# Every engine's program written out for all eight batches in place of a loop over two

## The reference

```python
xn = layernorm(x)
q, k, v = xn @ wq + bq, xn @ wk + bk, xn @ wv + bv      # 16 heads of 16
q, k = rope(q), rope(k)
s = softmax(q @ k.T / 4 + causal) @ v @ wo + bo
g = silu(ffn(xn))            # (silu(xn @ wg.T) * (xn @ wu.T)) @ wd.T, hidden size 768, int weights / 127
x = x + s * g
```

## Time and profile before

| | |
|---|---|
| time, median of 3 runs | 725.07 us (724.32 to 727.4) |
| the profiled execution, first to last instruction | 726.0 us |
| PE busy | 677.4 us, 93% |
| VectorE, ScalarE, GpSimd busy | 538.6, 411.4, 351.7 us |
| mean granted TensorE clock of that execution | 0.962 of full speed |

### The profile page before, as it was taken

How to read it: one execution, slowest core, us unless ns; L and a number is a source line. 1 busy time by engine, 2 the same in 40 slices (tenths; PEclk the granted TensorE clock), 3 DMA queues, 4 the chain that set the end, 5 groups by cost and what they waited for, 6 DMA issues and landing times.

```text
span 726.0 us, 15898 instructions
## 1 busy us (share of the span) xinstructions
PE 677.4 (93%) x4452; PEld 455.3 (63%) x4452; DVE 538.6 (74%) x1735; ACT 411.4 (57%) x897; POOL 351.7 (48%) x697
## 2 busy tenths in 40 slices
PE   1779999999999999899999999899999999999995
PEld 0656766676667665576656766568666766567653
DVE  3779678966978688675889669676697858886663
ACT  2446467756566447464476565555656644765671
POOL 1055493547625674336745476244762567422240
PEclk9888999999999999699999999879999999999898
DMA  8200000000100002000020001100020000100010
GB/s 247 78 1 1 31 1 1 2 3 1 62 28 1 1 1 89 6 1 2 1 89 2 2 1 59 35 2 3 1 74 16 1 1 2 60 1 1 1 60 29
DMA packets 16425, 18.15 MB, mean 25 GB/s; under 512 B 576, under 2 KB 15936, under 8 KB 16320
## 3 DMA queue, kind: packets, MB, share of 16 engines
q1 hardware_dynamic: 15232, 15.86, 6.8%
q10 hardware_dynamic: 1088, 1.05, 0.4%
HBM read 12.71 MB, written 4.19 MB: 23 GB/s over the span
## 4 chain that ended last, share of the span: by engine, by line
PE 84%; DVE 5%; issue 3%; ACT 3%; DMA 2%; POOL 1%; ACTq 0%; DVEq 0%; POOLq 0%
PE ps_w L487 34%; PE ps_w L565 12%; PE ps_w L554 12%; PE ps_o L580 11%; PE ps_w L536 7%; PE ps_w L542 3%; PE ps_w L589 3%; DMA rot<-L_attn_wo 2%; ACT probs L668 1%; PE ps_w L501 1%; ACT o_t L672 1%; DVE ps_w L778 1%; DVE h_lo L719 1%; PE ps_w L595 1%; DVE at_lo L801 1%
## 5 line engine op out<-in xcount | busy, mean ns | idle before, releaser
L778 DVE CUSTOM_DVE_ANT_0 ps_w<-ps_w,cst 128x512 f32<-128x512 f32 (+3 forms) x512 | 242.8, 509 | 54.5 <-PE ps_w L554 52.7
L668 ACT ACTIVATE probs<-ps_w 128x512 f32<-128x512 f32 (+1 forms) x384 | 194.1, 535 | 116.5 <-PE ps_w L565 113.6
L869 POOL TENSOR_SCALAR_AFFINE_SELECT probs<-probs 128x128 f32<-128x128 f32 (+1 forms) x384 | 130.7, 347 | 259.8 <-ACT probs L668 257.4
L565 PE MATMUL ps_w<-q_st,k_st 64*128 64x512 f32 (+3 forms) x512 | 137.9, 375 | 3.7 <-DVE at_lo L801 1.8
L554 PE MATMUL ps_w<-k_st,q_st 48*128 48x512 f32 (+3 forms) x512 | 139.3, 370 | 1.5 <-issue 0.8
L565 PEld LDWEIGHTS ps_w<-q_st,k_st 64*128 64x128 f32 x512 | 72.1, 189 | 52.9 <-issue 29.0
L658 ACT CAST q_st<-ps_w 128x512 fp32r<-128x512 f32 x128 | 74.6, 589 | 51.4 <-PE ps_w L542 39.3
L554 PEld LDWEIGHTS ps_w<-k_st,q_st 48*128 48x128 f32 x512 | 73.6, 189 | 47.3 <-issue 35.4
L487 PE MATMUL ps_w<-xt_hi,wgu_hi 128*128 128x512 f32 x192 | 89.3, 465 | 6.5 <-issue 4.8
L580 PE MATMUL ps_o<-probs,vals 128*32 128x512 f32 (+3 forms) x1024 | 92.5, 451 | 2.0 <-POOL probs L869 2.0
L487 PE MATMUL ps_w<-xt_lo,wgu_hi 128*128 128x512 f32 x192 | 80.7, 420 | 0.0
(11 more groups left out here) (91 smaller groups left out, 1178.2 us busy)
## 6 DMA issues: line engine op xcount, KB each, us to landing
xn<-L_attn_x SPq DMA_DIRECT2D x8, 512.0 KB, 4.8
res<-L_attn_x SPq DMA_DIRECT2D x8, 512.0 KB, 4.3
result<-res SPq DMA_DIRECT2D x8, 512.0 KB, 2.9
probs<-L_ffn_w_gate SPq DMA_DIRECT2D x1, 768.0 KB, 12.4
probs<-L_ffn_w_up SPq DMA_DIRECT2D x1, 768.0 KB, 14.2
probs<-L_ffn_w_down SPq DMA_DIRECT2D x1, 768.0 KB, 15.1
cst<-shape_constants SPq DMA_DIRECT2D x1, 384.0 KB, 5.1
rot<-L_attn_wq ACTq DMA_DIRECT2D x1, 256.0 KB, 4.2
```

The lines of the kernel that those rows point to most:

```text
L565: last = pe.matmul(dst[:, col:col + w], k_st[rows, pair % 4, kt * P:(kt + 1) * P], q_st2[rows, pair % 2, kt * P:SEQ], start=True, stop=True)
L668: nc.scalar.activation(probs[:, (pair % 2) * SLOTS + slot, col:col + WIDTH[c]], w_of(item)[:, 0:WIDTH[c]], ACT.Exp, scale=QSCALE).then_inc ...
L778: last = nc.vector.tensor_tensor_reduce(out=w_of(item)[:, col:col + w], in0=w_of(item)[:, col:col + w], in1=cst[:, C_MASK + SEQ - w:C_MASK ...
L869: nc.gpsimd.affine_select(out=v, in_=v, compare_op=ALU.is_ge, fill=0.0, base=0, pattern=pattern, channel_multiplier=-1).then_inc(masked_do ...
```

## The change

The program of each engine is written out for all batches: `run` goes through the prologue and batches 0 to 8 with no loop, and SyncE's loop is a Python loop as well. All waits are on constants, and the semaphores that were counted up apart are gone. The lists of items are the same items in the same order, with pair numbers written out in place of `AHEAD`. Working banks are handed out in turn, one after the other over the whole program, so that each is used again after exactly seven items. Three waits are new: VectorE before the first A of a pair (on `max_ready`), TensorE before the first U and G of batch 0 (on `xt_ready` and eight `wt_ready`), and before the first DN of batch 0 (all eleven `wt_ready`).

```diff
         def run(name, eng, do):
-
-            for item in plan(name, -1) + plan(name, 0):
-                do(item, None)
-            with eng.Fori(0, MIDDLE) as it:
-                for item in plan(name, 1) + plan(name, 2):
-                    do(item, it)
-            for item in plan(name, BATCH - 1) + plan(name, BATCH):
-                do(item, None)
+            for b in range(-1, BATCH + 1):
+                for item in plan(name, b):
+                    do(item)
...
-        def need(eng, s, value, per_batch, it, apart=None):
-
-
-
-            if it is not None:
-                assert value > 0
-                wait = eng.wait_ge(s, it * (2 * per_batch) + value)
-                if apart:
-                    wait.then_inc(apart, 1)
-            elif value > 0:
+
+        def need(eng, s, value):
+            if value > 0:
                 eng.wait_ge(s, value)
...
-            segment = plan("pe", b)
-            places = [i for i in (steps("pe", b) if b >= 0 else segment) if i[0] in WORK]
-            for item in segment:
+            for item in plan("pe", b):
                 if item[0] in WORK:
                     kind, first = item[0], WORK[item[0]][0]
-                    at = places.index(item) % WORK_BANKS
                     full[first] += 1
                     kinds[kind] = kinds.get(kind, 0) + 1
                     self.of[item] = (at, full[first], seen.get(at))
                     seen[at] = (kind, kinds[kind])
...
+                    at = (at + 1) % WORK_BANKS
...
-            with sp.Fori(1, BATCH - 1) as b:
+            for b in range(1, BATCH - 1):
...
                 elif kind in ("G", "U"):
-                    if kind == "G" and i == 0:
-                        need(pe, xt_ready, (b + 1) * KT, KT, it)
-                    dst = take_bank(item, it)
+                    if i == 0:
+                        need(pe, xt_ready, (b + 1) * KT)
+                        if b == 0:
+                            pe.wait_ge(wt_ready, 8)
+                    dst = take_bank(item)
...
                 elif kind == "DN":
-                    need(pe, h_ready, (b + 1) * HT, HT, it)
-                    dst = take_bank(item, it)
+                    need(pe, h_ready, (b + 1) * HT)
+                    if b == 0 and i == 0:
+                        pe.wait_ge(wt_ready, WT_USES)
+                    dst = take_bank(item)
...
                 elif kind == "A":
                     pair, c = divmod(i, CHUNKS)
                     m = b * PAIRS * CHUNKS + i
-                    wait_full(dve, "dve", item, it, apart=dve_passed)
+                    if c == 0:
+                        need(dve, max_ready, b * PAIRS + pair - 1)
+                    wait_full(dve, "dve", item)
```

More of the change, by code:

```diff
@@ new lines @@
+        QK:1> A:22 T2:2 PV:0 PV:1 A:23 T1k:4 B:11 AT:0< PV:2 A:24 B:12 B:13 A:25 AT:1< A:26 B:14 T1k:5 A:27 B:15
+        T1q:5 QK:2> PV:3 A:28 T2:3 B:16 B:17 A:29 B:18 A:30 V:2> T1q:6 B:19 QK:3> T2:4 B:20 A:31 B:21 T1k:6 B:22
+        A:32 V:3> A:33 OP:0< A:34 PV:4 B:23 A:35 OP:1< B:24 ON:0 B:25 PV:5 PV:6 B:26 A:36 B:27 T1q:7 T1k:7 A:37
+        A:38 A:39 T2:5 PV:7 B:28 A:40 A:41 B:29 ON:1 B:30 A:42 B:31 T1q:0> B:32 A:43 B:33 A:44 PV:8 T2:6 A:45
+        A:46 B:34 T1k:0> B:35 A:47 PV:9 A:0> B:36 B:37 G:0> A:1> A:2> PV:10 U:0> B:38 B:39 T1k:1> A:3> G:1> B:40
@@ L154 @@
+        PV:11 U:1> T2:7 T1q:1> A:4> A:5> B:41
     """,
     "act": """
[L156 to L162, removed]
@@ L164 @@
+        B:30 B:31 T1q:0> B:32 B:33 T2:6 B:34 T1k:0> B:35 B:36 G:0> B:37 B:38 T1k:1> HIq:2> B:39 G:1> B:40 T2:7
+        T1q:1> HL:0> PV:11 B:41
     """,
     "dve": """
[L166 to L170, removed]
@@ L188, in steps, with token_of @@
+        B:12 B:13 B:14 ROPE:8> B:15 ROPE:9> B:16 B:17 ROPE:10> B:18 B:19 ROPE:11> HIk:7 ROPE:12> ROPE:13> B:20
+        B:21 B:22 ROPE:14> ROPE:15> B:23 B:24 AD:0< HIk:0> B:25 B:26 B:27 AD:1< B:28 B:29 HIk:1> B:30 B:31 B:32
+        B:33 B:34 B:35 B:36 B:37 B:38 B:39 HIk:2> B:40 B:41
+    """,
+}
+def token_of(text):
+    kind, _, index = text.rstrip("<>").partition(":")
+    return kind, text.count(">") - text.count("<"), int(index or 0)
 def steps(engine, b):
[L190 to L199, removed]
@@ L200, in steps @@
-    return items
+    return [(kind, b + ahead, index) for kind, ahead, index in map(token_of, SCHEDULE[engine].split())]
 def plan(engine, b):
     if b < 0:
-        return [(kind, 0, int(index or 0)) for kind, _, index in (t.partition(":") for t in START[engine].split())]
+        return [(kind, ahead, index) for kind, ahead, index in map(token_of, START[engine].split())]
     return [item for item in steps(engine, b) if 0 <= item[1] < BATCH]
@@ L214, in __init__ @@
     def __init__(self):
-        self.of, full, kinds, seen = {}, {"act": 0, "dve": 0}, {}, {}
+        self.of, full, kinds, seen, at = {}, {"act": 0, "dve": 0}, {}, {}, 0
         for b in range(-1, BATCH + 1):
-            segment = plan("pe", b)
-            places = [i for i in (steps("pe", b) if b >= 0 else segment) if i[0] in WORK]
-            for item in segment:
+            for item in plan("pe", b):
                 if item[0] in WORK:
                     kind, first = item[0], WORK[item[0]][0]
-                    at = places.index(item) % WORK_BANKS
                     full[first] += 1
@@ L414, in rotate, with high_parts @@
             else:
-                need(eng, parts, parts_done, 3 * TT, it)
+                need(eng, parts, parts_done)
                 tensor_tensor(dst, dst, swapped, ALU.add).then_inc(rot_ready, 1)
-        def high_parts(name, eng, copy, passed, item, it):
+        def high_parts(name, eng, copy, item):
             kind, b, i = item
@@ L469, in _, with take_bank @@
             flag = {}
-            def take_bank(item, it):
+            def take_bank(item):
                 before = bank.of[item][2]
                 if before:
-                    need(pe, released[before[0]], before[1], bank.kind_per[before[0]], it)
+                    need(pe, released[before[0]], before[1])
                 return w_of(item)
@@ L538, in do @@
                 elif kind == "T2":
-                    need(pe, max_ready, n + 1, PAIRS, it)
-                    dst = take_bank(item, it)
+                    need(pe, max_ready, n + 1)
+                    dst = take_bank(item)
                     for tt in range(TT):
@@ L547, in do @@
                     if c == 0:
-                        need(pe, q_st_ready, b * PAIRS + pair + 1, PAIRS, it)
-                        need(pe, k_st_ready, b * PAIRS + pair + 1, PAIRS, it)
-                    dst = take_bank(item, it)
+                        need(pe, q_st_ready, b * PAIRS + pair + 1)
+                        need(pe, k_st_ready, b * PAIRS + pair + 1)
+                    dst = take_bank(item)
                     for h, qt, col in A_PARTS[c]:
@@ L559, in do @@
                     if c == 0:
-                        need(pe, q_st2_ready, b * PAIRS + pair + 1, PAIRS, it)
-                    dst = take_bank(item, it)
+                        need(pe, q_st2_ready, b * PAIRS + pair + 1)
+                    dst = take_bank(item)
                     for h, kt, col in B_PARTS[c]:
@@ L571, in do @@
                     if step == 0:
-                        need(pe, o_t_ready, g, GROUPS, it)
+                        need(pe, o_t_ready, g)
                         if group_ == 0:
-                            need(pe, v_ready, (b + 1) * TT, TT, it)
+                            need(pe, v_ready, (b + 1) * TT)
                     if step != 2:
-                        need(pe, masked_done, CHUNKS * (2 * g + 1) + (2, 4, 0, 6)[step], PAIRS * CHUNKS, it)
+                        need(pe, masked_done, CHUNKS * (2 * g + 1) + (2, 4, 0, 6)[step])
                     for hh in range(4):
@@ L632, in _, with do @@
         def _(act):
-            def do(item, it):
+            def do(item):
                 kind, b, i = item
@@ L659, in do @@
                 elif kind in ("HIq", "HIk"):
-                    high_parts("act", act, nc.scalar.copy, None, item, it)
+                    high_parts("act", act, nc.scalar.copy, item)
                 elif kind == "B":
@@ L663, in do @@
                     m = b * PAIRS * CHUNKS + i
-                    wait_full(act, "act", item, it)
+                    wait_full(act, "act", item)
                     if pair % 2 == 0 and c % 2 == 0:
-                        need(act, pv_done, TT * ((b * PAIRS + pair) // 2 - 1) + (1, 3, 4)[c // 2], TT * GROUPS, it)
+                        need(act, pv_done, TT * ((b * PAIRS + pair) // 2 - 1) + (1, 3, 4)[c // 2])
                     slot, col = slot_of(c)
```

206 lines of the change are left out of this document (99 added, 107 removed).

## The result

The changed kernel takes 707.57 us (706.97 to 710.02), against 725.93 us for the kernel before on the same chip: 0.975 of it, with a 95% interval of 0.970 to 0.980. The forecast was 708.0. A second set on another chip gave 708.53 us, 0.977 (0.969 to 0.985).

The account below looks back on a forecast made before the run. TensorE was taken as the bound; gains of 15.8 (back edges), 0 (register arithmetic), 0.3 (boundary banks) and 1.0 (tail banks) sum to 17.1 us, from the median 725.07 to 708.0 us, range 703 to 711.5.

Parts of the forecast that it names:

- Where the time went: Two long middle stretches, after batches 2 and 4: TensorE stops at the loop's way back, then runs at slow clock.
- Its size, 15.8 us: Removing the two back edges saves 8.02 + 7.75 us, stops plus slow clock; bounds 4.8 to 15.8.
- All on TensorE's path: The whole 15.8 us of the two back edges was taken to lie on TensorE's path.
- Register arithmetic, 0: Sequencers stop computing wait values from the loop counter; hidden behind TensorE's full queue, so 0 us gained.
- outer bound of 6.7 us: Most that constant waits could save: 0.08 of 5.9 us held throughout six batches of 82 us.
- the 81.7 us: Sign of being wrong: middle distances between landmarks under 81.7 us would mean register waits did cost.
- Banks at the boundary, 0.3 us: First five items of batches 1 to 7 no longer reuse banks after five items: 0.3 us gained (0 to 1).
- Banks in the tail, 1.0 us: Batches 7 and 8: three TensorE bank waits (A:17, B:8, ON:2) shrink or go, 1.0 us gained (0 to 1.4).
- The tail's clock, taken as 0: Three half-clock tail stretches, together 13.6 us, taken as unchanged: 0 us, bounds −3 to +6.8.
- New waits, 0: VectorE's wait on `max_ready` and TensorE's new batch 0 waits are already met or covered by slack: 0 us.
- Starving: Rival: straight code's instruction blocks arrive late, each costing TensorE 8 us; slower, up to 756 us; chance 0.03.
- The dips stay: Rival: middle clock dips remain and only the gaps go, 6.1 us gained, 719 us; chance 0.06.

Follow-up runs that it names:

- body written three times: The kernel before with its two-batch loop body written three times, each in a single-turn loop, so no engine goes back: 712.7 us, ratio 0.985.
- far jump: The changed kernel with an always-taken TensorE branch over 400 matmuls that never run, ahead of batches 3 and 5: 725.0 us, ratio 0.998.
- near jump: The changed kernel with an always-taken TensorE branch over 24 matmuls that never run, ahead of batches 3 and 5: 707.6 us, ratio 0.978.
- VectorE alone in the loop: The kernel before with TensorE, ScalarE and GpSimd written out and VectorE (and SyncE) still looping: 728.4 us, ratio 1.002.
- old banks: The changed kernel with bank numbers restarting at each batch again: 713.8 us, ratio 0.983, middle stretches 81.65 us.
- the changed one once more: The changed kernel unchanged, run again for a second trace and more times: 708.53 us.
- TensorE alone in the loop: The kernel before with VectorE, ScalarE and GpSimd written out and TensorE (and SyncE) still looping: 724.8 us, ratio 0.999.

## Why the prediction was right, point by point

*Where the time went.* Right. Both long stretches ended, with no stop and at full clock, and the experiments show the cause: no way back, no price (body written three times); a far jump, the price again; a near jump, none.

*Its size, 15.8 us.* Right for this pair of profiles, where the difference is 15.8. As a price for the kernel it is some 3 us too high: with nothing but the ways back gone the median fell by 12.9 us (body written three times). Two clean ways back cost 6.4 us, and the slow clock behind them is there or not; both profiled ones had it in full, 11 us of the 15.8. Over all runs the clock's part in the whole change is 8.6 us at most. The bounds named were 4.8 and 15.8; the lower one, the stops alone, missed the 0.9 us of waiting for VectorE that a slow clock hides.

*"All on TensorE's path."* The wrong step. The prediction took TensorE's own stop as the price, with nothing on the other engines that TensorE waits for, and didn't name VectorE's stop beside it (3.5 us in that trace). With VectorE alone in the loop the time is 728.4 us all the same, and TensorE waits 2.0 and 0.8 us for it: a way back on either of these two engines is enough to hold TensorE. Had only TensorE's program been written out, the forecast by that reasoning would have been some 709 us, and it is 728.

*Register arithmetic, 0.* Right (0.1 us in a batch at most, 0.6 in all). But the separate counted waits, which go with it, were not costed at all: 0.5 us in each of six stretches, 3 us. They had been lumped with work that has slack. VectorE does have 17 us of slack in a batch, and the instruction ahead of each A item shows all the same. A likely reason is that TensorE waits for single maxima to get its banks back; the traces don't show which wait it is. The outer bound of 6.7 us for cheaper waits covered it. The stretches came out under the 81.7 us that the prediction named as the sign that the register arithmetic did cost, and the sign pointed at the wrong cause.

*Banks at the boundary, 0.3 us.* 0.15 us a batch by the old banks' stretches, 0.9 in all: at the upper end of the bound (0 to 1).

*Banks in the tail, 1.0 us.* This pair of profiles doesn't show it, since the clock differs. The waits of TensorE that changed, from 622 us on:

```profile
PE ps_o L502 <- POOL probs L797: 1.2, 2, 0.6
...
PE ps_w L409 <- ACT probs L594: 0.5, 1, 0.5
...
PE ps_w L487 <- DVE gate L755: 0.2, 1, 0.2
```

Compare. B:8 waits 0.2 in place of 0.7 us for the gate, and ON:2's wait for a bank is gone. A:17's 0.5 us has moved to DN:0 behind it, as the prediction warned. But waits for GpSimd's masks grew from 0.4 to 1.2 us, and the list's total is 5.5 us in both.

The whole tail, from the last landmark to the end, in the kernel before, the changed one and the changed one once more (columns as in the earlier trace rows):

```profile
573.98:726.00 152.02, 139.38 (x967) 93.10 (x966) 102.32 (x338) 84.62 (x186) 58.21 (x135) 0.95 0.06 19
```

```profile
555.01:708.30 153.29, 140.94 (x967) 94.58 (x966) 101.77 (x338) 84.29 (x186) 58.48 (x135) 0.92 0.06 18
```

```profile
558.67:708.10 149.43, 136.98 (x966) 91.45 (x966) 101.69 (x338) 83.83 (x186) 58.10 (x135) 0.95 0.06 19
```

At the clock that the kernel before had, 0.95, the changed tail takes 149.4 us; the near and the far jump, which have the same tail, give 149.6 and 149.3. The body written three times, with the old banks and counted waits, has 151.9 at 0.95. So the tail did get some 2.5 us shorter, and 1.0 for the banks isn't refuted. How much of it is banks, counted waits or where in the tail the low clock fell is open.

*The tail's clock, taken as 0.* In this trace it went the other way. The profiled tail is 1.3 us longer at 0.92 in place of 0.95 of full clock, worth some 4.7 us (153.29 × 0.08 − 152.02 × 0.05) and so outside the bound of −3. After the wait that stayed, the clock was low for 13.6 us, against 3.4 there before:

```profile
656.90:670.50 13.60, 13.60 (x63) 8.52 (x55) 7.10 (x28) 6.98 (x16) 3.16 (x10) 0.50 0.00 1
```

*New waits, 0.* Nothing in the trace speaks against it; VectorE's busy time is 64.9 us a batch, and the stretches are shorter.

*The rivals.* Starving doesn't happen: 40 blocks are read, and behind the prologue the chain of neither trace of the changed kernel has a piece of "issue" over 0.6 us. "The dips stay" is refuted for the middle of the profiled run: 519 us at full clock on end are fine.

So the forecast is right within 0.5 us, and that close it is luck. The main term has the right cause, but its clock half is a property of one profile and makes it some 3 us too large for the median. Against that stand some 3 us of counted waits that were put at nothing. Between the two profiles the same waits, 3.4 us with the banks, were met by a tail 2.3 us longer than forecast, by its clock.

## What to carry to other kernels

Where several engines each run a long loop body, look at the way back on every engine that feeds or empties the bound one, not only on the bound one; writing out one of them alone can give nothing. Branches over a short piece of code are free here; branches to far code are not, in a loop or out of it. Work on an engine with slack isn't free for that reason alone: wait instructions of their own on VectorE, which has 17 us of slack in a batch, cost 0.5 us in each batch.

## What the runs showed of the hardware that was not expected

- After a stop of TensorE of 2.0 to 2.5 us the clock falls to half for some 13.6 us, or only for 3.4, or not at all: in the loop kernels twice in full, once for 3.4 us and once not at all (before, two traces), once in full and once not at all (TensorE alone in the loop), and twice in full or longer in the far jump. Without a stop the middle batches show single slow stretches of 3.4 us now and then. What decides it is open.
- A way back stops TensorE 2.2 to 2.5 us and VectorE 2.6 to 3.5 us.
- Register arithmetic in TensorE's sequencer, some 80 instructions in a batch, costs nothing that can be seen while its queue is full.
